# Narrow attention heads on 32-row tiles, their rows gathered through DRAM, and weighted values placed tile by tile

## The chip, the cores and the metric

The kernel runs on one core of a Trainium2 chip. TensorE (PE) multiplies matrices; its weight loads are shown as an engine of their own, PEld. VectorE (DVE), ScalarE (ACT) and GpSimd (POOL) do elementwise work and reductions, SyncE (SP) issues the DMAs. The metric is the device time of one execution in microseconds, lower is better.

## The reference

Four transformer blocks run one after the other on `x` (8 batch elements of 256 tokens of width 128), each with self attention, cross attention to a context of 1601 tokens of width 96, and a feed-forward layer. Blocks 0 and 2 have 16 heads of width 64 ("wide"), blocks 1 and 3 have 16 heads of width 8 ("narrow").

```python
def _attend(q, k, v):                      # block 1; block 3 is alike
    sim = jnp.einsum('bhid,bhjd->bhij', q, k) * HD ** (-0.5)
    attn = jax.nn.softmax(sim, axis=-1)
    out = jnp.einsum('bhij,bhjd->bhid', attn, v)
...
x = x + (_attend(h1 @ Wqkv ...) @ W_proj + b_proj)             # self, 256 keys
x = x + (_attend(h2 @ W_q, ctx @ W_k, ctx @ W_v) @ W_out + b_out)   # cross, 1601 keys
x = x + (gelu(h3 @ W_fc1 + b_fc1) @ W_fc2 + b_fc2)
```

## The kernel before

**Layers and units.** The layers have numbers 0 to 11; attention layers are 0, 1, 6, 7 (wide) and 3, 4, 9, 10 (narrow); 0, 3, 6, 9 are self attention, the others cross attention. Batch elements are taken in pairs (four pairs), and for each layer first the one, then the other. An attention layer of one element is split into units: two wide heads or four narrow heads each, so 8 or 4 units. Keys come in tiles of 128 (2 or 13 of them, the last with 65 rows), and two tiles make a pair. What precedes the units of an element in a layer (projection, norm, feed-forward, keys and queries) is its prelude.

**A unit.** First the jobs "max": the products of queries and keys, in pieces of 400 or 401 keys for cross attention, go to a bank of `ring` (three PSUM banks), and DVE takes each row's maximum into `max_part` (L2042). "shift" turns the maxima into rows that are added inside the score product. Then, chunk by chunk, PE writes `scores` (keys x queries), ScalarE takes the exponential into `probs` (L1719, `exps`), and PE multiplies by the values into `o_acc` (`weigh_values`). ScalarE copies `o_acc` to `attn` at the unit's end ("close"). For wide heads GpSimd adds up the weights (L1271, `add_weights`), for narrow ones a column of ones in the values does.

**Narrow heads.** Queries and keys are held as fp16 high and low halves (`split_of`). A unit's 128 rows in `nk` and `nq` are four blocks of 32 rows: the shift, high x high, low x high, high x low, each with 4 heads x 8 dimensions. SyncE fills blocks 1 to 3 with six DMAs per unit (L1134, L1137, "expand"). GpSimd multiplies the queries by a mask of each head into `qm` (L1290, "mask"), so that a product over all 128 rows gives one head. A score matmul has 128 rows and 512 columns: two heads at once. After "shift" ScalarE copies the shift row into `qm` four times (L1695, `shift_queries`). A chunk is a pair of tiles of two heads.

**Values.** `weigh_values(n, pair)` is one step for a pair of tiles: the heads of a unit go to 32 or 64 columns of the array each, 4 x 2 or 2 x 2 matmuls in fp32, which the trace shows as two instructions each.

**Order of the work.** `make_order` gives each step a due time, and `Plan` replays the steps with assumed durations (`part(engine, stream, due, what, dur, deps, lat)`): each engine takes the due step that is ready. The result is a fixed order for each engine (`ORDER_OF`) and the banks of `ring`. Every engine then runs its list in order.

Of the kernel before, what the change touches and what calls it, by code (L numbers as in the profile page):

```python
# [13 lines left out]
P = 128  # L14
B, N, D = 8, 256, 128
M, DC = 1601, 96
H = 16
# [10 lines left out]
NK_SLOTS, QM_SLOTS, VS_SLOTS = 3, 2, 4  # L28
# [3 lines left out]
class Attention:  # L32
# [170 lines left out]
def make_order():  # L203

    out = []
    begins, ends, expanded, values_at, scores_at, scored, done = {}, {}, {}, {}, {}, {}, {}
# [5 lines left out]
    def place_prelude(s, u, begin):  # L212
# [6 lines left out]
        for m in order:  # L219
# [5 lines left out]
            if kind == "keys" and ATT[s].cross and u % 2:  # L225
                at = max(at, expanded[s, u - 1] + 3.0)
            at += {("ctx", 4): 6.0, ("hn", 1): 5.0, ("ffout", 0): 2.5}.get((kind, j), 0.0)
            put(at, "pre", s, u, m)
            at += AFTER[kind] + (5.0 if kind == "project" and BEFORE[s].wide else 0.0)
# [22 lines left out]
    def place_jobs(un):  # L252
# [6 lines left out]
        if not t.wide:  # L259
# [4 lines left out]
            expanded[t.sub, un.u] = expand  # L264
            put(expand, "expand", n)
            mask = max(expand + 4.5, floor)
            put(mask, "mask", n)
            floor = mask + 0.5
# [45 lines left out]
    for un in UNITS:  # L314
# [48 lines left out]
class Plan:  # L363
# [4 lines left out]
    def __init__(self, static):  # L368
# [3 lines left out]
        for time, i, one in static:  # L372
            place = {"pre": self.pre, "job": self.job, "scores": self.scores, "values": self.values,
                     "close": self.close, "scale": self.scale, "copy": self.copy, "expand": self.expand,
                     "mask": self.mask}[one[0]]
# [6 lines left out]
    def chunk_parts(self, g):  # L382
        un, c = CHUNKS[g]
        out = [("PE", ("values", un.n, c // un.t.halves))]
        if un.t.wide:
            out.append(("POOL", ("values", un.n, c)))
        return out

    def pre(self, due, one):
# [37 lines left out]
        elif kind == "src":  # L427
            old = last_of(s - 3, u - u % 2 + 1)
            on("PE", 0.7, ("PE", ("values", old.n, old.t.pairs - 1)))
            on("ACT", 0.62, pe)  # L430
        elif kind in ("keys", "queries"):
# [3 lines left out]
            spread = [("SP", ("expand", last_of(s, u - 1).n - k)) for k in range(NK_SLOTS)] \  # L435
                if kind == "keys" and t.cross and u % 2 and j == 0 else []
# [68 lines left out]
    def wide_job(self, due, one, un, t, n, j, kind, i, k, pe):  # L505
# [30 lines left out]
        elif kind == "val":  # L536
            back = 2 if t.cross else VS_SLOTS
            deps = self.inputs(un) if i == 0 else []
            if at >= back:
                old = self.wide[at - back]  # L540
                deps.append(("PE", ("values", old.n, old.t.pairs - 1)))
# [7 lines left out]
        else:  # L549
            self.part("PE", "sum", due, one, 0.55, [("POOL", ("values", n, t.pairs - 1))], 0.2)  # L550
# [3 lines left out]
    def narrow_job(self, due, one, un, t, n, j, kind, i, k, pe):  # L554
        if kind == "max":
            self.part("PE", "max", due, one, 0.21 if t.cross else 0.3, [("POOL", ("mask", n)), ("SP", ("expand", n))], 0.2)
# [6 lines left out]
        self.part("PE", "shift", due, one, 0.55, [("DVE", one)], 0.2)  # L563
        self.part("ACT", "shift", due, one, 1.6, [pe])
# [1693 lines left out]
```

## Time and profile before

| | |
|---|---|
| median of 3 runs | 7116.8 us (7109.58 to 7126.71) |
| profiled execution | 7129.41 us, span 7127.6 us |
| PE busy | 6424.0 us, 90% |
| DVE, ACT, POOL busy | 69%, 56%, 38% |
| mean granted TensorE clock | 0.956 |
| moved by DMA | 204.00 MB, 29 GB/s |

A line of the timeline or of a group names the kernel line, the engine, the operation, the tile written and the tiles read, and the shape; for matmuls "128*32" is rows by columns of the array in use. L1309 is the helper `mm` through which nearly all matmuls go, L1593 the copy helper of ScalarE, so such lines are told apart by their tiles: `scores<-qm,nk` are narrow scores, `ring<-nk,qm` the products for narrow maxima, `scores<-qop,...` wide scores, `o_acc<-probs,...` weighted values. Lengths of single matmuls hold the time through the array, and they overlap; the pace is the time from start to start.

### The profile page before, as it was taken

Reading aid. Unit: us, or ns where it says so; the run is one execution under the profiler, and the core shown is the slowest. Engines: PE = TensorE matmul, PEld = TensorE weight load, DVE = VectorE, ACT = ScalarE, POOL = GpSimd, SP = SyncE. Lnnn points to the kernel's source line nnn. Section 1 sums busy time; section 2 is a strip of 40 time slices with the busy share of each in tenths; the row PEclk is TensorE's granted clock in tenths of the full one; section 3 lists DMA queues with packets and bytes.
Section 4 is the critical chain, followed back from the end, with each engine's and each line's share of the span. In section 5 each row is a group of like instructions: output and inputs, shape, how many; then the busy total and the mean of one; then the engine's idle time right before and its main releaser. Section 6 shows DMA issues by size and latency. Waiting matters only on the chain.

```text
span 7127.6 us, 119830 instructions
## 1 busy us (share of the span) xinstructions
PE 6424.0 (90%) x43254; PEld 3725.9 (52%) x43254; DVE 4929.0 (69%) x9886; ACT 3981.7 (56%) x7106; POOL 2707.1 (38%) x2326
## 2 busy tenths in 40 slices
PE   6899889989889998998988999899897999989988
PEld 4555445653455544565455554556444555346644
DVE  6777666657777766665777776666577776766656
ACT  4454565655545557565654555756474445565656
POOL 2446114651144611565014551156401455116630
PEclk9999999999999999999999999999999999999999
DMA  3101011100111001111011100111001010011100
GB/s 81 33 25 26 22 27 32 28 27 18 44 32 27 25 21 31 29 30 29 12 46 31 29 24 20 33 28 30 26 16 46 25 30 24 18 35 28 29 18 11
DMA packets 347633, 204.00 MB, mean 29 GB/s; under 512 B 165006, under 2 KB 319982, under 8 KB 346927
## 3 DMA queue, kind: packets, MB, share of 16 engines
q1 hardware_dynamic: 347054, 196.34, 10.7%
q8 instruction: 357, 5.85, 0.3%
q14 instruction: 222, 1.81, 0.1%
HBM read 105.18 MB, written 1.05 MB: 15 GB/s over the span
## 4 chain that ended last, share of the span: by engine, by line
PE 68%; DVE 12%; ACT 9%; POOL 6%; issue 4%; SPq 1%; DVEq 0%; POOLq 0%; DMA 0%; ACTq 0%
PE ring L1309 34%; PE o_acc L1309 17%; PE scores L1309 16%; DVE max_part L2042 6%; POOL weight_sum L1271 4%; ACT qop L1593 4%; ACT probs L1719 2%; DVE region L2004 1%; DVE o_inv L2073 1%; DVE ring L2021 1%; ACT qm L1593 1%; ACT region L1593 1%; DVE ring L2018 1%; POOL qm L1290 1%; PE ring L1405 1%
## 5 line engine op out<-in xcount | busy, mean ns | idle before, releaser
L2042 DVE TENSOR_REDUCE max_part<-ring 128x1 f32<-128x400 f32 (+2 forms) x4608 | 2454.9, 578 | 829.4 <-PE ring L1309 813.8
L1719 ACT ACTIVATE probs<-scores 128x1024 f32<-128x1024 f32 (+1 forms) x2048 | 1917.6, 969 | 1231.0 <-PE scores L1309 845.3
L1271 POOL TENSOR_TENSOR weight_sum<-weight_sum,probs 128x512 f32<-128x512 f32 (+1 forms) x1408 | 1785.7, 1268 | 143.5 <-ACT probs L1719 2.4
L1309 PE MATMUL o_acc<-probs,region 128*32 128x256 f32 (+2 forms) x13312 | 1360.1, 389 | 0.0
L1271 POOL TENSOR_TENSOR weight_sum<-probs 128x512 f32<-128x512 f32 x256 | 324.8, 1269 | 2125.9 <-PE ring L1309 1794.1
L1593 ACT ACTIVATE region<-ring 64x400 f16<-64x400 f32 (+4 forms) x1744 | 815.0, 477 | 520.5 <-PE ring L1309 416.4
L1309 PEld LDWEIGHTS o_acc<-probs,region 128*32 128x32 f32 (+2 forms) x13312 | 589.0, 123 | 534.0 <-issue 317.9
L1593 ACT ACTIVATE qop<-ring 64x256 f16<-64x256 f32 (+1 forms) x1536 | 563.4, 375 | 446.9 <-DVE ring L2021 278.8
L1309 PE MATMUL scores<-qop,region 128*128 128x256 f16 (+1 forms) x3328 | 781.6, 275 | 12.6 <-ACT probs L1719 8.1
L1309 PE MATMUL ring<-nk,qm 128*128 128x400 f16 (+2 forms) x2560 | 720.6, 343 | 79.2 <-DVE max_part L2042 42.6
L1309 PE MATMUL scores<-qop,x_cop 128*128 128x256 f16 (+1 forms) x3328 | 778.0, 274 | 0.0
L1290 POOL TENSOR_TENSOR qm<-nq,head_mask 128x1024 f16<-128x1024 f16 x128 | 242.1, 1894 | 1129.1 <-PE scores L1309 981.3
L1309 PE MATMUL ring<-region,qop 128*128 128x400 f16 (+1 forms) x2048 | 592.2, 342 | 81.1 <-DVE max_part L2042 46.4
L2004 DVE TENSOR_TENSOR region<-ring,region 64x400 f16<-64x400 f32 (+1 forms) x1024 | 590.5, 577 | 98.8 <-ACT region L1593 74.7
L1309 PE MATMUL scores<-qm,nk 128*128 128x512 f16 (+1 forms) x1920 | 564.9, 385 | 34.7 <-ACT probs L1719 24.5
L2073 DVE RECIPROCAL o_inv<-ring 128x256 f32<-128x256 f32 x256 | 449.8, 1757 | 105.2 <-PE ring L1309 96.3
L1309 PEld LDWEIGHTS ring<-nk,qm 128*128 128x128 f16 x2560 | 222.2, 98 | 571.6 <-DVE max_part L2042 313.3
L1309 PE MATMUL ring<-src_t,stage 96*128 96x400 f32 (+1 forms) x1024 | 439.3, 525 | 33.5 <-ACT qop L1593 32.8
L1309 PEld LDWEIGHTS ring<-region,qop 128*128 128x128 f16 x2048 | 186.7, 98 | 415.7 <-issue 329.7
L1309 PE MATMUL ring<-h_t,stage 128*128 128x256 f32 x1152 | 349.3, 409 | 50.3 <-DVE max_part L2042 10.6
L1309 PEld LDWEIGHTS scores<-qop,region 128*128 128x128 f16 (+1 forms) x3328 | 330.1, 99 | 123.5 <-ACT probs L1719 37.8
L1309 PEld LDWEIGHTS scores<-qop,x_cop 128*128 128x128 f16 (+1 forms) x3328 | 331.3, 100 | 94.1 <-issue 39.8
(159 smaller groups left out, 7449.6 us busy)
## 6 DMA issues: line engine op xcount, KB each, us to landing
x_cop<-region SPq DMA_DIRECT2D x256, 200.1 KB, 3.1
stage<-in_wide SPq DMA_DIRECT2D x512, 64.0 KB, 2.0
nk<-region SPq DMA_DIRECT2D x192, 100.1 KB, 2.2
stage<-in_wide SPq DMA_DIRECT2D x128, 128.0 KB, 2.6
v_stage<-in_wide SPq DMA_DIRECT2D x256, 64.0 KB, 1.8
wo_stage<-in_wide SPq DMA_DIRECT2D x32, 512.0 KB, 4.0
cop_few<-kop_few SPq DMA_DIRECT2D x256, 32.0 KB, 1.9
ff_w<-in_ff_w SPq DMA_DIRECT2D x24, 256.0 KB, 3.1
```

The source lines that it names most:

```text
L1271: pool.tensor_tensor(total, before, probs[0:rows_, g % PROBS, at:at + BANK], ALU.add)\
L1290: pool.tensor_tensor(qm[:, un.narrow_at % QM_SLOTS, :, :], nq[:, z, :].unsqueeze(1).broadcast_to([P, 4, N]), head_mask[:, :].unsqueeze(2). ...
L1309: return pe.matmul(out, lhs, rhs, start=start, stop=stop, skip_group_check=True)
L1405: last = pe.transpose(out[:, p * P:(p + 1) * P], attn[:, p, j * P:(j + 1) * P], ident)
L1593: return act.activation(out, src, ACT.Identity, **kw)
L1719: act.activation(to, src, ACT.Exp, scale=t.scale).then_inc(exp_done.sem, 1)
L2004: last = dve.tensor_tensor(kop[other, h, a0:a0 + w], v[part, 0:w], kop[part, h, a0:a0 + w], ALU.subtract)
L2018: dve.tensor_tensor(v, v, rope_sin[:, a0:a0 + w], ALU.mult).then_inc(rope_step.sem, 1)
L2021: dve.tensor_tensor(v, v, products, ALU.add).then_inc(rope_step.sem, 2)
L2042: dve.tensor_reduce(dst, src, AX.X, ALU.max).then_inc(*release(one))
L2073: dve.reciprocal(o_inv[:, un.wide_at % 2, :], ring[:, bank(one), 0:N]).then_inc(*release(one))
```

## The change

1. A narrow unit's rows are now ordered by head: four heads of 32 rows, each with its four blocks of 8. Each prelude writes its keys and queries to a scratch in DRAM (`key_rows`, `query_rows`; the step "spill", three DMAs each), and "expand" reads a unit's 128 rows from there with two DMAs. The shift blocks of the scratch are written once at the start.
2. A maximum's product and a score product use one head's 32 rows of `nk` and `nq`. Scores of one head fill one bank, so a score step has four matmuls of 256 columns for what were two of 512. The heads of the maxima now change fastest.
3. The mask on GpSimd and `qm` are gone. The shift is added to the queries by three matmuls (a copy of `nq` and the maxima), and ScalarE writes `nq` back in one copy.
4. `weigh_values(n, k)` is a step for one tile of keys, for wide heads too; the adding on GpSimd is a step of its own.
5. Keys of the second element of a pair wait for the spill of the first one's, not for its last "expand". Some assumed durations of `Plan` are new.

```diff
-        out = [("max", (h, q), k) for g in (0, 2) for q in range(QT) for k in range(len(self.kc)) for h in (g, g + 1)]
+        out = [("max", (h, q), k) for q in range(QT) for k in range(len(self.kc)) for h in range(4)]
...
-            put(values_at[n, pair], "values", n, pair)
+            for k in t.tiles(pair):
+                put(values_at[n, pair], "values", n, k)
+            if t.wide:
+                put(values_at[n, pair], "add", n, pair)
...
-            self.part("PE", "max", due, one, 0.21 if t.cross else 0.3, [("POOL", ("mask", n)), ("SP", ("expand", n))], 0.2)
+            self.part("PE", "max", due, one, 0.12 if t.cross else 0.2, [("SP", ("expand", n))], 0.25)
...
-        self.part("PE", "scores", due, one, (0.45 if t.wide else 0.23) * tiles, deps, 0.2)
+        self.part("PE", "scores", due, one, (0.45 if t.wide else 0.13) * tiles, deps, 0.2)
...
-        tiles = len(t.tiles(pair))
-        self.part("PE", "values", due, one, 0.53 * tiles, deps, 0.25)
+        self.part("PE", "values", due, one, 0.53, deps, 0.25)
...
+                    elif one[0] == "spill":
...
+                        rows_ = (query_rows if of_queries else key_rows)[int(t.cross), u % 2, :, :]
+                        rows_ = rows_.rearrange("(h b r) k -> b h r k", b=4, r=8)
+                        for block_, half in zip((1, 2, 3), (0, 0, 1) if of_queries else (0, 1, 0)):
+                            sp.dma_start(rows_[block_, :, :, 0:w], src[:, half, 0:w]).then_inc(done.sem, 16)
...
-                        for block_, of_k, of_q in ((1, 0, 0), (2, 1, 0), (3, 0, 1)):
-                            to = slice(32 * block_, 32 * block_ + 32)
-                            sp.dma_start(nq[to, z, :], q[part, of_q, :]).then_inc(nq_in[z].sem, 16)
-                        for block_, of_k, of_q in ((1, 0, 0), (2, 1, 0), (3, 0, 1)):
-                            to = slice(32 * block_, 32 * block_ + 32)
-                            sp.dma_start(nk[to, z, 0:un.t.keys], k[part, of_k, 0:un.t.keys]).then_inc(nk_in[z].sem, 16)
+                            wait((queries_kept.sem, queries_kept.at((s, u), 48)))
+                            wait((keys_kept.sem, keys_kept.at((s, u), 48)))
+                        part = slice(P * un.p, P * un.p + P)
+                        sp.dma_start(nq[:, z, :], query_rows[int(un.t.cross), u % 2, part, :]).then_inc(nq_in[z].sem, 16)
+                        sp.dma_start(nk[:, z, 0:un.t.keys], key_rows[int(un.t.cross), u % 2, part, 0:un.t.keys])\
+                            .then_inc(nk_in[z].sem, 16)
...
+            wait((init_step, 3))
+            for many in range(2):
+                for z in range(2):
+                    for to, src, w in ((key_rows, nk, MP), (query_rows, nq, N)):
+                        rows_ = to[many, z, :, :].rearrange("(h b r) k -> b h r k", b=4, r=8)
+                        sp.dma_start(rows_[0, :, :, :], src[:, 0, 0:w]).then_inc(blank_in, 16)
...
-                        for q in range(QT):
-                            last = mm(out[0:32, q * P:(q + 1) * P], max_cols[:, q, :], ident, True, True)
+                        mm(out[:, 0:N], ident_half[:, :], nq[:, z, :], True, False)
+                        for q in range(QT):
+                            last = mm(out[:, q * P:(q + 1) * P], max_cols[:, q, :], ident_part[:, :], False, True)
...
-                            last = mm(out[:, m * w:(m + 1) * w], qm[:, un.narrow_at % QM_SLOTS, h, qq * P:(qq + 1) * P],
-                                      nk[:, z, a0:a0 + w], True, True)
+                            last = mm(out[:, m * w:(m + 1) * w], nq[part, z, qq * P:(qq + 1) * P], nk[part, z, a0:a0 + w],
+                                      True, True)
...
-                            last = mm(scores[0:r, first + k % 2, :], nk[:, un.narrow_at % NK_SLOTS, k * P:k * P + r],
-                                      qm[:, un.narrow_at % QM_SLOTS, 2 * half:2 * half + 2, :], True, True)
+                            for h in range(2):
+                                part = slice(64 * half + 32 * h, 64 * half + 32 * h + 32)
+                                at = (k % 2) * N
+                                last = mm(scores[0:r, first + h, at:at + N], nk[part, slot, k * P:k * P + r], nq[part, slot, :],
+                                          True, True)
...
-                    for h in range(4):
-                        last = copy(qm[0:32, un.narrow_at % QM_SLOTS, h, :], ring[0:32, bank(one), 0:N], scale=head_part[0:32, h:h + 1])
-                    last.then_inc(*release(one))
+                    copy(nq[:, un.narrow_at % NK_SLOTS, :], ring[:, bank(one), 0:N]).then_inc(*release(one))
```

The order of PE in a steady narrow cross unit, first before. `ring<-nk,qm` is the product for a maximum, `scores<-qm,nk` half of a score step, `o_acc<-probs,region` weighted values (x8: two tiles of four heads).

```order
L1309 MATMUL o_acc<-probs,region 32x256 x8
L1309 MATMUL ring<-nk,qm 128x400 x3
L1309 MATMUL scores<-qm,nk 128x512 x2
L1309 MATMUL ring<-nk,qm 128x400
L1309 MATMUL scores<-qm,nk 128x512 x2
L1309 MATMUL ring<-nk,qm 128x401
L1309 MATMUL o_acc<-probs,region 32x256 x8
```

And with the change, where `nq` stands for `qm`:

```order
L1318 MATMUL o_acc<-probs,region 32x256 x4
L1318 MATMUL ring<-nk,nq 128x401
L1318 MATMUL o_acc<-probs,region 32x256 x4
L1318 MATMUL ring<-nk,nq 128x401
L1318 MATMUL scores<-nq,nk 128x256 x4
L1318 MATMUL ring<-nk,nq 128x400
L1318 MATMUL scores<-nq,nk 128x256 x4
L1318 MATMUL ring<-nk,nq 128x400
L1318 MATMUL o_acc<-probs,region 32x256 x4
```

The values of a pair now stand as two blocks of one tile, with a maximum's product between them, and a score step is one group of four matmuls.

The order of PE in a unit of the second wide cross layer (7), before and with the change; `ring<-region,qop` are products for wide maxima, the next rows belong to the following units.

```order
L1309 MATMUL o_acc<-probs,region 64x256 x4
L1309 MATMUL ring<-region,qop 128x400
L1309 MATMUL ring<-h_t,stage 128x256
L1309 MATMUL ring<-ctx_t,stage 128x401
L1309 MATMUL ring<-ident,pair_cols 65x128 x2
```

```order
L1318 MATMUL o_acc<-probs,region 64x256 x2
L1318 MATMUL ring<-region,qop 128x400
L1318 MATMUL o_acc<-probs,region 64x256 x2
L1318 MATMUL ring<-h_t,stage 128x256
L1318 MATMUL ring<-ctx_t,stage 128x401
```

Here too a pair's block of four is cut in two by a maximum's product.

The order of SyncE's DMAs where a narrow self layer (3) ends and the cross layer (4) begins, before and with the change.

```order
L1134 DMA nq<-q_split 32x256 x3
L1137 DMA nk<-k_few 32x256 x3
L1134 DMA nq<-q_split 32x256 x3
L1137 DMA nk<-region 32x1601 x3
```

```order
L1137 DMA key_rows<-region 16x8x1601 x3
L1149 DMA nq<-query_rows 128x256
L1150 DMA nk<-key_rows 128x256
L1137 DMA query_rows<-q_split 16x8x256 x3
L1149 DMA nq<-query_rows 128x256
L1150 DMA nk<-key_rows 128x1601
```

The long keys now go out ahead of the last self unit's rows, and the queries go out and come back before the first cross unit's rows are there.

## Rows read from the trace of the kernel before

**Rows 1.** Page, part 1: busy time, share and instructions of each engine.
```profile
PE 6424.0 (90%) x43254; PEld 3725.9 (52%) x43254; DVE 4929.0 (69%) x9886; ACT 3981.7 (56%) x7106; POOL 2707.1 (38%) x2326
```

**Rows 2.** Windows: stretch, its length, then each engine's busy time; granted clock; DMA.
```profile
1993.30:2486.90 493.60, 456.79 (x2924) 279.43 (x2922) 379.38 (x730) 242.99 (x427) 262.76 (x219) 0.99 0.11 28
2486.90:2559.30 72.40, 57.33 (x383) 34.46 (x381) 30.86 (x70) 42.44 (x86) 22.88 (x21) 0.89 0.13 32
2559.30:2772.90 213.60, 201.19 (x1502) 86.17 (x1502) 150.84 (x322) 140.43 (x215) 16.16 (x16) 0.95 0.06 15
2772.90:2888.30 115.40, 98.51 (x616) 63.32 (x616) 82.31 (x154) 71.38 (x163) 28.63 (x32) 0.93 0.17 47
2888.30:3292.40 404.10, 392.24 (x2756) 259.03 (x2755) 263.63 (x474) 239.68 (x419) 266.46 (x220) 0.98 0.11 28
...
2654.50:2674.80 20.30, 19.70 (x168) 7.86 (x168) 16.45 (x34) 14.42 (x20) 1.90 (x1) 1.00 0.09 21
3005.30:3096.40 91.10, 91.10 (x659) 60.02 (x657) 63.45 (x113) 59.22 (x105) 63.47 (x53) 1.00 0.11 28
```

**Rows 3.** Groups by line and shape: busy, mean ns | idle before, releasers.
```profile
L1309 PE MATMUL scores<-qm,nk 128*128 128x512 f16 x1792 | 524.0, 386 | 34.6 <-ACT probs L1719 24.5 <-ACT qm L1593 8.1
L1309 PE MATMUL ring<-nk,qm 128*128 128x400 f16 x1536 | 491.9, 360 | 38.5 <-DVE max_part L2042 19.6 <-DVE ff_h L1918 1.8 <-DVE qop L2001 1.7
L1309 PE MATMUL o_acc<-probs,region 128*32 128x256 f32 x6144 | 411.3, 385 | 0.0
L1309 PEld LDWEIGHTS ring<-nk,qm 128*128 128x128 f16 x2560 | 222.2, 98 | 571.6 <-DVE max_part L2042 313.3 <-issue 127.8 <-POOL qm L1290 27.3
```

**Rows 4.** Timeline of PE in a steady narrow cross unit: start, length, instruction.
```profile
961.03 0.59 PE L1309 MATMUL scores<-qm,nk 128*128 128x512 f16 x2
961.47 0.33 PE L1309 MATMUL ring<-nk,qm 128*128 128x400 f16 x1
961.73 1.07 PE L1309 MATMUL o_acc<-probs,region 128*32 128x256 f32 x16
962.73 0.69 PE L1309 MATMUL ring<-nk,qm 128*128 128x400 f16 x3
963.26 0.59 PE L1309 MATMUL scores<-qm,nk 128*128 128x512 f16 x2
```

**Rows 5.** Timeline of PE, a block of values with one tile.
```profile
2485.84 0.65 PE L1309 MATMUL o_acc<-probs,region 65*64 65x256 f32 x4
2486.42 0.61 PE L1309 MATMUL scores<-qm,nk 128*128 128x512 f16 x2
```

**Rows 6.** Timeline of PE, a matmul of one row behind a maximum.
```profile
2585.95 0.34 PE L1309 MATMUL ring<-nk,qm 128*128 128x400 f16 x1
2586.23 0.71 PE L1309 MATMUL ring<-rows,ones 1*128 1x128 f32 x4
```

**Rows 7.** Timeline of ScalarE and of PE at the end of a narrow unit.
```profile
971.93 1.53 ACT L1593 ACTIVATE qm<-ring,head_part 32x256 f16<-32x256 f32 x4
...
973.52 1.04 PE L1309 MATMUL scores<-qm,nk 128*128 128x512 f16 x4 [0.20 <-ACT qm L1593]
```

**Rows 8.** DMA issues: KB each, median us from issue to landing.
```profile
nk<-region SPq DMA_DIRECT2D x192, 100.1 KB, 2.2
wo_stage<-in_wide SPq DMA_DIRECT2D x32, 512.0 KB, 4.0
```

**Rows 9.** Timeline of SyncE's queue and of PE, first narrow cross unit.
```profile
2550.53 1.98 SPq L1134 DMA_DIRECT2D nq<-q_split  x3
...
2560.30 17.28 PE L1309 MATMUL ring<-nk,qm 128*128 128x401 f16 x36
```

**Rows 10.** Timeline of SyncE's queue after the start.
```profile
43.07 0.90 SPq L1071 DMA_DIRECT2D stage<-in_wide  x2
44.73 1.20 SPq L1119 DMA_DIRECT2D cop_few<-kop_few  x2
```

**Rows 11.** Windows: the stretch with maxima alone.
```profile
2559.30:2580.00 20.70, 19.08 (x47) 5.24 (x47) 18.72 (x41) 1.24 (x5) 0.14 (x1) 0.58 0.08 18
```

More of the change, by code:

```diff
@@ L372, in __init__ @@
         for time, i, one in static:
-            place = {"pre": self.pre, "job": self.job, "scores": self.scores, "values": self.values,
+            place = {"pre": self.pre, "job": self.job, "scores": self.scores, "values": self.values, "add": self.add,
                      "close": self.close, "scale": self.scale, "copy": self.copy, "expand": self.expand,
-                     "mask": self.mask}[one[0]]
+                     "spill": self.spill}[one[0]]
             place((time, i), one)
@@ L383, in chunk_parts @@
         un, c = CHUNKS[g]
-        out = [("PE", ("values", un.n, c // un.t.halves))]
+        out = [("PE", ("values", un.n, un.t.tiles(c // un.t.halves)[-1]))]
         if un.t.wide:
-            out.append(("POOL", ("values", un.n, c)))
+            out.append(("POOL", ("add", un.n, c)))
         return out
@@ L434, in pre @@
             on("PE", 0.7 if kind == "keys" and t.cross else 0.45, *deps)
-            spread = [("SP", ("expand", last_of(s, u - 1).n - k)) for k in range(NK_SLOTS)] \
-                if kind == "keys" and t.cross and u % 2 and j == 0 else []
+            spread = [("SP", ("spill", s, u - 1, 0))] if kind == "keys" and t.cross and u % 2 and j == 0 else []
             on("ACT", 0.62 if kind == "keys" and t.cross else 0.5, pe, *spread)
@@ L549, in wide_job @@
         else:
-            self.part("PE", "sum", due, one, 0.55, [("POOL", ("values", n, t.pairs - 1))], 0.2)
+            self.part("PE", "sum", due, one, 0.55, [("POOL", ("add", n, t.pairs - 1))], 0.2)
             old = [("POOL", ("scale", self.wide[at - 2].n))] if at >= 2 else []
@@ L562, in narrow_job @@
         self.part("DVE", "shift", due, one, 0.2, maxima + ([("PE", ("job", old.n, old.t.shift_job))] if old else []))
-        self.part("PE", "shift", due, one, 0.55, [("DVE", one)], 0.2)
-        self.part("ACT", "shift", due, one, 1.6, [pe])
+        self.part("PE", "shift", due, one, 0.7, [("DVE", one)], 0.2)
+        self.part("ACT", "shift", due, one, 0.4, [pe])
     def scores(self, due, one):
@@ L585, in values @@
     def values(self, due, one):
-        _, n, pair = one
+        _, n, k = one
         un = UNITS[n]
         t = un.t
-        deps = [("ACT", ("scores", un.chunk + pair * t.halves + k)) for k in range(t.halves)]
-        if pair == 0:
+        pair = k // 2
+        deps = [("ACT", ("scores", un.chunk + pair * t.halves + half)) for half in range(t.halves)]
+        if k == 0:
             if t.wide:
@@ L611, in close @@
         un = UNITS[n]
-        deps = [("PE", ("values", n, un.t.pairs - 1))]
+        deps = [("PE", ("values", n, un.t.kt - 1))]
         if un.p == 0 and n:
@@ L625, in copy, with spill @@
         self.part("SP", "copy", due, one, 1.4, [("ACT", ("job", un.n, un.t.last_op))], 2.2)
+    def spill(self, due, one):
+        _, s, u, of_queries = one
+        kind = "queries" if of_queries else "keys"
+        self.part("SP", "spill", due, one, 2.1, [("DVE", ("pre", s, u, of_kind(s, kind)[-1]))], 2.2)
     def expand(self, due, one):
         un = UNITS[one[1]]
-        deps = []
+        s, u = un.t.sub, un.u
+        deps = [("SP", ("spill", s, u, k)) for k in range(2)]
         if un.narrow_at >= NK_SLOTS:
@@ L632, in expand @@
             deps.append(("PE", ("scores", old.chunk + old.t.chunks - 1)))
[L633 to L644 removed]
+        self.part("SP", "expand", due, one, 1.4, deps, 2.2)
     def run(self):
@@ L1716, in exps @@
                         to, src = to[0:r, :, :], src[0:r, :, :]
+                    elif not t.wide:
+                        to, src = to[0:r, :, 0:N], src[0:r, :, 0:N]
                     else:
```

162 lines of the change are left out of this document (74 added, 88 removed).

## The prediction

> **What bounds the kernel now.** I read the page first: TensorE (PE) is busy 90% of 7127.6 us, the next engine, VectorE (DVE), 69% [rows 1]. A share says little about single stages, so next comes the busy time by stage, for the second of four pairs of batch elements [rows 2]. The two cross attentions with wide heads take 493.6 and 404.1 us of it and PE has work for 456.8 and 392.2; in the last row, four units of 22.8 us, PE is busy all the time. A cross attention with narrow heads takes 213.6 us, PE busy 201.2; there are two a pair, so eight in all, with eight units each. In its steady unit of 20.3 us PE is busy 19.7 us and DVE 16.45 us in 34 instructions, 32 of them maxima. That is the floor of such a unit if PE gets cheaper.
>
> Then the parts of a narrow unit on PE. 1792 matmuls of 512 columns (and 128 for the last, short tile) make scores, most of the others feed the maxima with 400 columns [rows 3]. The timeline gives the pace: two score matmuls take 0.44 us to the next start, so 0.215 each, three for maxima 0.53, so 0.17 to 0.18 each, and a block of values of 16 instructions (four heads, two passes of fp32, two tiles of keys) 1.00 us [rows 4]. The four heads overlap: 6144 instructions of mean 385 ns cover 411.3 us [rows 3]. A block costs more than its columns. From the last maximum (0.17) to the block it is 0.26 us: entering the 32-column form costs 0.09 [rows 4]. A block with one tile takes 0.58 us [rows 5], one with two 1.00. So a block cut in two costs 2 x 0.58 - 1.00 + 0.09 = 0.25 us; the one-tile block shown has 64-column tiles, and I use 0.24. Work on 32 rows or fewer has the same entry price: a maximum followed by a matmul of one row is 0.28 us away, not 0.17 [rows 6].
>
> **The change part by part, on PE.**
> (a) Scores of narrow heads. A tile's two heads were one matmul over 128 rows and 512 columns; now they are two matmuls over 32 rows and 256 columns, in different row tiles and PSUM banks. No row of before shows row tiles side by side. Bounds: they overlap as the column tiles do, and a pair costs half, 0.11 for 0.215; or not at all, and it stays 0.22. I take the first, as the nearest row, the four column tiles, does so. 64 units x 26 tile-halves = 1664 matmuls: -1664 x 0.107 = -178 us. The two-tile stages (256 more) are paced by chains, below.
> (b) Values by single tiles. In the order of PE's instructions I count blocks of values: 447 before and 724 after in the narrow cross stages, 816 and 1024 in the wide cross stages, 128 and 228 in the wide self stages, 64 and 76 in the narrow self stages. +277 x 0.24 = +66 us narrow cross; +208 x 0.24 = +50 us wide cross.
> (c) Changes between 32-row work and full-array work (preludes, shifts, the next wide unit's operands): changes of form rise from 3186 to 4920; the blocks of (b) explain 2 x 597 = 1194 of them, of the other 540 some 464 lie in the narrow cross stages: x 0.09 = +42 us.
> (d) Shift of a narrow unit: four instructions of 128 columns become one of 256 more (+0.11 x 64 = +7 us).
> PE in the narrow cross stages: -178 + 66 + 42 + 7 = -63 us.
>
> **What goes beside PE.** ScalarE's four copies after the shift, 1.53 us, become one over 128 rows with as many columns, 0.38 to 0.45. The next scores start right after those copies (0.20 us idle, put down to them) [rows 7], so up to 1.1 us per narrow unit can go, 70 us over 64 units; PE has other work in most of these holes, and I take half, -34. GpSimd's mask goes: the weight loads of maxima waited 27.3 us for it in the whole run [rows 3]; I take -17. Matmuls for maxima next to scores of another row tile can overlap too (up to 0.17 each), but DVE's 16.45 per unit is close below; bounds 0 and, at the floor in all units, -96 more; I take none. Narrow cross: -63 - 34 - 17 = -114 us, or 1.8 per unit: the steady unit goes from 20.3 to 18.5 us, still above 16.45.
> In the wide cross stages nothing pays for (b): the four units at 22.8 us have no hole [rows 2], so the 124 cuts of the second layer count in full (+30), of the first one (84 cuts, PE busy 93%) about half (+10). The wide self stages, PE busy 85% [rows 2]: half of 100 x 0.24, +12.
> Narrow self stages (one takes 72.4 us, PE busy 57.3 [rows 2]): PE waits for chains there. Cheaper: the mask and the copies on ScalarE, and the six issues of SyncE for a unit's rows, 0.6 us each, become two. Dearer: before the first unit the rows go out (three issues, 1.8 us, a landing of 2.2) and in again. Old chain for the first unit: 3.7 of issues + 2.2 of landing, 5.9 us; new one: 1.8 + 2.2 + 1.2 + 2.2 = 7.4, so +1.5 us; with keys of 410 KB the last landing is nearer the 4.0 of a 512 KB one [rows 8], 9.2 in all. In the cross stage that chain starts at 2550.53 and PE's first maximum was at 2560.30, after a turn [rows 9]: 9.8 us hide it. The spill of long keys (3 x 410 KB) also stands in SyncE's order just ahead of the last narrow self unit's rows, which may come 5 us late once per pass and layer (8 x 5 = 40 at worst, 0 at best). I set gains of 3 us per stage against a loss of 3: 0, with -40 and +40 as bounds.
> Start: SyncE reaches its program at 43.07 us and the copy that the first scores need at 44.73 [rows 10]. Eight issues more, at 0.6 to 1.2 each, come ahead of it: +7 us (bounds 5 to 10).
>
> **Sum** against the profiled execution of 7129.4 us: -114 + 40 + 12 + 0 + 7 = -55. That execution is 0.18% above the median of the three runs, 7116.8; 55 less than the median is **7062 us**.
>
> **Two rules of the Trainium skill.** The weight loads of these matmuls took 98 ns, hidden behind matmuls of 170 to 215 ns [rows 3]; now two of them are wanted in 109. The Trainium skill (TensorE: Matmul & The Clock Gate, section "LDWEIGHTS (loading the stationary operand)") says that a load costs by its columns and as much for 32 rows as for 128. By that, were the loads serial, (a) would shrink to nearly nothing; that is rival A. The Trainium skill also says (same page, "Part 3: Packing small matmuls") that loads and matmuls of different row groups overlap, and gives 3.07 times for four row tiles; by that (a) stands. No row of before decides between them.
>
> **Rivals.**
> A, row tiles don't overlap (serial weight loads, or writes to PSUM that exclude each other). For it: nothing in before shows two row tiles at once. Against: 32-column loads and matmuls do overlap. Then (a) is 0 and all switches stay: -55 + 178 = +123, 7240 us, slower. It decides once a pair of 256-column score matmuls takes over 0.14 us: (a) is then 1664 x 0.074 = 123, and the sum 0. Chance 0.15.
> B, the clock falls in the narrow cross stages. In the 20.7 us with only maxima, of 400 columns per 0.485 us, the granted clock was 0.58, between the two levels 1.2 and 2.4 GHz, against 1.00 in the steady unit [rows 2, 11]. Now more of the stage is such thin work on a quarter of the rows. PE's some 17 us of a unit would nearly double at the low level: +16 us; in a third of 56 units +300, 7360 us. Against it: values and scores still stand between, and PE stays busy most of the time. Chance 0.05.
> C, the gain is eaten: DVE is late for each maximum, PE stands in single waits between forms, and the wide cross cuts cost all of their 50. Then narrow cross gives only PE's -63, and the sum is -63 + 50 + 12 + 7 = +6: 7123 us, no change. Chance 0.10.
> D, more than forecast: maxima overlap with scores and the narrow units run at DVE's floor, about 17 us: -96 more, 6966 us. Chance 0.12.
> My forecast, -20 to -100, has 0.58.
>
> **Numbers.** Within 0.2% (14 us), about what a measurement of this kernel can tell from no change: C's 0.10 and little else. Faster: forecast 0.58 + D 0.12 = 0.70, less a bit for the forecast's upper edge: 0.69. Slower: A 0.15 + B 0.05 + 0.01. Together 0.69 / 0.10 / 0.21. The range for 8 in 10 goes down to D with some of what the self stages may add, 6950, and up into the nearer side of A, where tiles overlap in part, to 7200.
>
> **What would show it.** In the profile after: the steady narrow cross unit at 18 to 19 us with DVE over 85% busy; score matmuls of 256 columns in pairs starting some 5 ns apart, a chunk of four in 0.22 us (0.44 by A); two blocks of values per pair of tiles, each 0.55 to 0.6 us; the wide cross stage of 404.1 us longer by some 7 us; granted clock of the steady unit 1.00 (B: under 0.9). The forecast is wrong if the narrow cross stages don't get shorter by 8 us or more each, or if a wide stage grows by more than 15.

## The result

| | median, us | lowest to highest | runs |
|---|---|---|---|
| before | 7121.76 | 7109.58 to 7128.62 | 4 |
| after | 7239.66 | 7229.06 to 7258.08 | 4 |

The ratio is 1.017, 95% interval 1.0144 to 1.0197: the change makes the kernel 118 us slower. The forecast was 7062, its range ended at 7200. The profiled execution of after took 7258.08 us, span 7256.3 us; it is the slowest of its four.

### The profile page after: what moved, and what is told of

Same layout as the page of the kernel before. It is cut to its first block, busy times and chain, and to the rows that moved or that the text cites. A ratio compares the mean times of both kernels' runs of the same rounds, so it can differ in the third digit from the quotient of the medians.

```text
span 7256.3 us, 123089 instructions
## 1 busy us (share of the span) xinstructions
PE 6571.5 (91%) x45302; PEld 3660.9 (50%) x45302; DVE 4929.7 (68%) x9884; ACT 3832.7 (53%) x6722; POOL 2465.1 (34%) x2199
## 4 chain that ended last, share of the span: by engine, by line
PE 69%; DVE 12%; ACT 9%; issue 5%; POOL 4%; SPq 1%; DVEq 0%; POOLq 0%; DMA 0%; ACTq 0%
PE ring L1318 34%; PE o_acc L1318 20%; PE scores L1318 13%; DVE max_part L2056 6%; ACT qop L1614 4%; POOL weight_sum L1294 3%; ACT probs L1736 3%; DVE ring L2035 1%; ACT region L1614 1%; DVE ring L2032 1%; PE ring L1414 1%; DVE o_inv L2087 1%; DVE region L2018 1%; DVE qop L2015 1%; PE ring L1406 0%
## 5 line engine op out<-in xcount | busy, mean ns | idle before, releaser
L1318 PE MATMUL o_acc<-probs,region 128*32 128x256 f32 (+2 forms) x13312 | 1571.4, 432 | 0.0
L1318 PE MATMUL ring<-nk,nq 32*128 32x400 f16 (+2 forms) x2560 | 773.0, 395 | 67.9 <-DVE max_part L2056 42.3
L1318 PEld LDWEIGHTS o_acc<-probs,region 128*32 128x32 f32 (+2 forms) x13312 | 551.1, 129 | 555.0 <-issue 427.6
L1318 PEld LDWEIGHTS ring<-nk,nq 32*128 32x128 f16 x2560 | 199.7, 97 | 717.7 <-issue 333.5
L1257 POOL TENSOR_TENSOR var<-mv,eps 128x2 f32<-128x2 f32 x96 | 18.7, 195 | 1495.5 <-DVE mv L1828 1495.5
L1318 PE MATMUL scores<-nq,nk 32*128 32x256 f16 (+1 forms) x3840 | 383.5, 326 | 33.3 <-ACT probs L1736 20.0
L2015 DVE TENSOR_TENSOR qop<-ring,qop 64x256 f16<-64x256 f32 x512 | 215.5, 421 | 281.7 <-ACT qop L1614 277.6
```

The costliest lines, as they stand in the source:

```text
L1257: pool.tensor_tensor(var[:, :], mv[:, :, 1], eps[:, 0:QT], ALU.add).then_inc(var_ready.sem, 1)
L1318: return pe.matmul(out, lhs, rhs, start=start, stop=stop, skip_group_check=True)
L2015: last = dve.tensor_tensor(qop[part, z, 2 + h, :], v[part, 0:N], qop[part, z, h, :], ALU.subtract)
```

## The profile after

Windows of the kernel after, second pair of batch elements, first the stages of the layers 1, 3, 4, 6 and 7 as in [rows 2], then the eight units of the first of the two narrow cross stages. Columns: stretch, length, busy time of PE, PEld, DVE, ACT, POOL, granted clock, DMA share, GB/s.

```profile
2032.70:2530.40 497.70, 463.92 (x2937) 279.24 (x2934) 379.12 (x731) 244.18 (x426) 260.24 (x218) 0.99 0.11 29
2530.40:2602.70 72.30, 59.47 (x408) 35.75 (x407) 29.53 (x68) 32.19 (x63) 6.71 (x12) 0.76 0.20 58
2602.70:2823.30 220.60, 205.92 (x1680) 77.00 (x1681) 148.33 (x312) 124.31 (x173) 3.31 (x8) 0.76 0.08 24
2823.30:2944.90 121.60, 103.07 (x657) 63.62 (x655) 86.27 (x166) 79.51 (x182) 29.84 (x33) 0.96 0.18 47
2944.90:3347.90 403.00, 394.17 (x2765) 254.17 (x2764) 262.69 (x473) 236.68 (x416) 262.36 (x218) 0.99 0.11 29
...
2602.70:2656.90 54.20, 53.57 (x269) 18.45 (x270) 36.19 (x77) 19.20 (x30) 1.12 (x4) 0.62 0.09 27
2656.90:2682.40 25.50, 24.22 (x215) 8.76 (x213) 17.38 (x37) 15.50 (x26) 0.41 (x1) 0.80 0.21 60
2682.40:2704.80 22.40, 20.94 (x196) 7.28 (x195) 17.61 (x36) 13.35 (x17) 0.00 (x0) 0.77 0.08 24
2704.80:2725.40 20.60, 19.33 (x194) 6.66 (x193) 16.62 (x34) 13.36 (x17) 0.00 (x0) 0.83 0.08 25
2725.40:2753.80 28.40, 26.99 (x219) 11.82 (x218) 18.68 (x44) 16.95 (x23) 0.89 (x2) 0.76 0.07 23
2753.80:2781.20 27.40, 24.16 (x215) 9.13 (x215) 18.35 (x42) 14.73 (x18) 0.89 (x2) 0.75 0.00 1
```

The narrow cross stage, 213.6 us at clock 0.95 in [rows 2], now takes 220.6 at 0.76. The clock has two levels, so a mean of 0.76 is 2 x (1 - 0.76) = 48% of the stretch at 1.2 GHz: 106 us, where it was 22 ("low time" below, taken from the clock's own records and so a little off what the rounded column gives). The steady unit, clock 1.00 before, has 0.77 to 0.83.

Added up over the four pairs, with the stages bounded by the last copy of `o_acc` of each:

| kernel | narrow cross, us (low) | narrow self | wide cross | wide self |
|---|---|---|---|---|
| before | 1692 (155) | 617 (126) | 3593 (111) | 1204 (219) |
| after | 1782 (858) | 615 (254) | 3604 (87) | 1235 (203) |
| difference | +90 | -2 | +11 | +31, of it 7 at the start |

The narrow cross stages carry 90 of 131 us. Stage times are those of one profiled execution of each kernel, and executions of one kernel lie 19 us (before) and 29 us (after) apart, so differences of a few us say little. How one unit looks inside is in the timeline of PE, 12 us of the kernel after; columns: start, length, instruction, and in brackets the idle time before it and what ended it.

```profile
2705.34 0.82 PE L1318 MATMUL ring<-nk,nq 32*128 32x401 f16 x2 [0.50 <-DVE max_part L2056]
...
2707.92 1.70 PE L1318 MATMUL ring<-nk,nq 32*128 32x400 f16 x4
...
2710.64 1.94 PE L1318 MATMUL o_acc<-probs,region 128*32 128x256 f32 x16
2712.51 0.52 PE L1318 MATMUL ring<-nk,nq 32*128 32x400 f16 x2
...
2716.18 0.64 PE L1318 MATMUL o_acc<-probs,region 128*32 128x256 f32 x8
2716.75 0.34 PE L1318 MATMUL ring<-nk,nq 32*128 32x401 f16 x1
2717.02 0.64 PE L1318 MATMUL o_acc<-probs,region 128*32 128x256 f32 x8
2717.59 0.34 PE L1318 MATMUL ring<-nk,nq 32*128 32x401 f16 x1
2717.60 0.39 PE L1318 MATMUL scores<-nq,nk 32*128 32x256 f16 x4
2717.83 0.33 PE L1318 MATMUL ring<-nk,nq 32*128 32x400 f16 x1
```

This is where one unit passes into the next. In the first two rows shown PE gives the next unit's first maxima, on 32 rows, from 2708.14 on one per 0.48 us at the pace of DVE, with scores beside them. At 2708.6 the clock falls and stays low to 2715.4. In between a block of 16 lasts 1.87 us to the next start; it was 1.00 in [rows 4]. From 2716 on, at the upper level, everything has its forecast price: a block of one tile 0.57 us, 0.27 from a maximum to a block, four score matmuls in 0.23. So row tiles do overlap, and a maximum overlaps with scores too (starts at 2717.59 and 2717.60). The Trainium skill (TensorE: Matmul & The Clock Gate, section "Part 3: Packing small matmuls") says that matmuls on different row groups overlap. The trace agrees: four score matmuls on two row tiles take 0.23 us, where the forecast had 0.44 if tiles did not overlap.

That the thin maxima between two units lose the clock is the suspicion with which the experiments begin.

## Experiments

All times are medians, each beside runs of the kernel before on the same chip (7116.5 to 7120.5 us in the three sets). Theory 1: products for maxima on 32 rows lose the clock. Rivals: the cuts of the values and their changes of form (theory 2 below); the plan's new durations; too few columns rather than too few rows.

**e1, values by pairs again.**
```diff
-            for k in t.tiles(pair):
+            for k in t.tiles(pair)[-1:]:
                 put(values_at[n, pair], "values", n, k)
```
(The PE step then places both tiles.)

> The changed kernel with the values placed by pairs of tiles again (one step of TensorE holds both tiles), everything else kept. Theory 1, the clock: the changed kernel is slow because TensorE stands at its lower level for 858 us of the eight narrow cross stages (155 before), and that comes from the products for the maxima, which are not touched here. Then the time at the lower level stays above 1100 us in the whole run (1413 now), the narrow cross stages (1782 us in all) lose at most the 66 us of the cuts, the wide cross stages (3604 us) some 10 to 40 us, and the time is 7150 to 7200. Theory 2, the cuts: 597 blocks of values more and the changes of form around them are what costs. Then the narrow cross stages come back to 1690 or less, and the time to under 7120, whatever the clock does.

Measured 7163.8, ratio to before 1.0059 (1.0044 to 1.0074). The time and the low time of the whole run, 1269 us, are as theory 1 has them; but the narrow cross stages fell by 96 us, to 1686, more than the 66 it allowed, and to just what theory 2 asked for (whose time, under 7120, it missed). Their low time fell by 185 us as well, so this run does not part the two. What it does show is that in the changed kernel the cuts cost 96 us: with pairs, and all maxima still on 32 rows, the narrow cross stages are back where the kernel before has them (1692). The wide cross stages lost 8 us.

**e2, maxima over 128 rows again**, with the mask of queries on GpSimd; scores, single tiles and scratch stay.
```diff
-                            last = mm(out[:, m * w:(m + 1) * w], nq[part, z, qq * P:(qq + 1) * P], nk[part, z, a0:a0 + w],
+                            last = mm(out[:, m * w:(m + 1) * w], qm[:, un.narrow_at % QM_SLOTS, h, qq * P:(qq + 1) * P],
+                                      nk[:, z, a0:a0 + w],
                                       True, True)
...
-            self.part("PE", "max", due, one, 0.12 if t.cross else 0.2, [("SP", ("expand", n))], 0.25)
+            self.part("PE", "max", due, one, 0.21 if t.cross else 0.3, [("POOL", ("mask", n))], 0.2)
```
The second hunk is in the plan: a maximum has its duration of before again and waits for the mask. So PE's order of work is not quite that of the changed kernel (699 blocks of values in the narrow cross stages, not 724).

> The changed kernel with the products for the narrow maxima over all 128 rows of the array again, against queries masked by head on GpSimd; scores on 32 rows, values by single tiles and the scratch are kept. Theory 1, the clock (products over 32 rows, paced by VectorE, do not hold the clock, products over 128 rows do): the time at the lower level in the narrow cross stages falls from 858 us to under 250, and these stages from 1782 us to 1600 to 1680; the time is 7060 to 7150. Theory 2, the cuts: the stages stay at 1780 or grow by the mask and by more changes of form, 7240 to 7300.

Measured 7071.1, ratio 0.9929 (0.9913 to 0.9946): as theory 1 has it, 169 us under the changed kernel, and faster than before, though it adds GpSimd's mask and a change of form at each maximum. Low time in the narrow cross stages 213 us for 858, the stages 1635 us for 1782. Windows of this kernel, the stage and two steady units:

```profile
2550.30:2750.00 199.70, 189.70 (x1692) 71.90 (x1691) 150.13 (x315) 126.81 (x178) 15.95 (x15) 0.95 0.08 23
...
2620.00:2641.30 21.30, 20.20 (x196) 6.55 (x195) 17.97 (x38) 13.39 (x16) 1.89 (x1) 1.00 0.09 27
2641.30:2661.10 19.80, 19.27 (x193) 6.36 (x193) 16.47 (x34) 13.39 (x16) 1.90 (x1) 1.00 0.08 24
```

**e3, each product for a narrow cross maximum twice, on 32 rows.** **e4, one more over 128 rows ahead of each.** In e4 the added line is as below; e3 adds the 32-row product a second time.
```diff
+                            if t.cross:
+                                mm(out[:, m * w:(m + 1) * w], nq[:, z, qq * P:(qq + 1) * P], nk[:, z, a0:a0 + w], True, True)
                             last = mm(out[:, m * w:(m + 1) * w], nq[part, z, qq * P:(qq + 1) * P], nk[part, z, a0:a0 + w],
```

> The changed kernel with each 400-column product for a narrow cross maximum issued twice, both times on 32 rows, into the same bank (the second overwrites the first). If the rows in use decide the clock, the lower level keeps over 700 us of the narrow cross stages, and the time grows by up to 32 x 0.17 us per unit, 7300 to 7600. If it is how many columns pass, or how much of the time TensorE is busy, with 32 rows as good as 128, twice the columns lift the clock: under 300 us at the lower level, and a time of 7150 to 7300, as the second product costs 0.17 us at the upper level and is partly beside VectorE's 0.48.

> The changed kernel with one more 400-column product over all 128 rows ahead of each narrow cross maximum, into the same bank, which the right one on 32 rows overwrites. If the rows in use decide the clock: under 250 us at the lower level in the narrow cross stages (858 now), steady granted clock 0.95 to 1.00 there. The price is TensorE's own: 0.17 us and a change of form of 0.09 to 0.19 us for each of 2048, so 530 to 740 us less what lies in VectorE's shadow: 7300 to 7700. If the rows do not matter, the clock is as in the kernel with the thin product issued twice.

Measured 7466.1 and 7830.7 (one run each). e3 came out as the rows in use would have it: low time 1047 us in the narrow cross stages, so twice the columns on 32 rows don't lift the clock. e4 missed its expectation, with 899 us of low time and a time above the range; its units say more. Windows of e3, units 2 to 4 of the first element, layer 4:

```profile
2714.00:2737.80 23.80, 23.35 (x246) 8.91 (x245) 17.50 (x35) 15.44 (x26) 0.20 (x1) 1.00 0.21 65
2737.80:2764.80 27.00, 26.34 (x230) 9.29 (x229) 17.73 (x35) 13.44 (x16) 0.00 (x0) 0.68 0.07 17
2764.80:2787.00 22.20, 21.54 (x229) 7.95 (x225) 16.76 (x34) 13.50 (x17) 0.00 (x0) 0.85 0.08 24
```
And of e4, the same units and then the units 2 and 3 of the second element, last this unit 3 in the third pair of batch elements:

```profile
2819.90:2849.50 29.60, 29.29 (x242) 11.22 (x241) 18.53 (x35) 15.72 (x26) 0.00 (x0) 1.00 0.15 47
2849.50:2877.40 27.90, 27.90 (x230) 9.72 (x229) 19.16 (x35) 13.58 (x17) 0.00 (x0) 1.00 0.06 19
2877.40:2904.20 26.80, 26.80 (x227) 9.36 (x226) 18.07 (x33) 13.54 (x17) 0.00 (x0) 1.00 0.04 9
...
2934.70:2980.90 46.20, 44.80 (x246) 13.28 (x245) 19.82 (x40) 15.24 (x17) 0.89 (x2) 0.61 0.00 1
2980.90:3028.80 47.90, 47.90 (x232) 11.89 (x232) 20.22 (x36) 13.99 (x16) 0.00 (x0) 0.50 0.00 1
...
4919.80:4948.20 28.40, 28.40 (x233) 9.90 (x232) 19.71 (x36) 13.54 (x16) 0.00 (x0) 1.00 0.01 1
```

In e4 the three units hold 1.00 throughout, here and in all but one of the eight stages. e3 and e4 keep the order of the changed kernel and add the same number of columns, so they compare well. In the units 2 to 4 of the eight stages together the low time is 256 us in the changed kernel, 273 in e3 and 87 in e4. But in e4, once the clock has fallen, it can stay down, for 47.9 us in which PE is busy all the time; the same unit at the upper level took 28.4. So added work over 128 rows kept a clock that was up in these units, and did not bring back one that was down. In e4 PE also has less idle time than in e3, so e4 alone would not show that it is the rows; e2 points the same way with no column added, though in another order of work.

**e5, e2 with pairs.** The edit of e1 on e2.

> The kernel with products for the narrow maxima over 128 rows (7071.1 us), and its values placed by pairs of tiles again. If a block of values cut in two costs TensorE 0.24 us wherever TensorE is the bound, the narrow cross stages (1635 us) lose 20 to 66 us and the wide cross stages (3601 us) 20 to 50: 6960 to 7030. If single tiles cost nothing because they fill waits (the wide cross stages lost only 8 us when the pairs came back to the changed kernel): 7060 to 7085. If pairs are worse, since a longer step of TensorE holds up a product for a maximum: over 7085.

Measured 7072.7, ratio 0.9933 (0.9918 to 0.9948), the middle case in total, but not for its reason: the narrow cross stages became 28 us shorter (1607) and the narrow self stages 2, the wide self stages 27 us longer and the wide cross stages 2. Beside e1 it gives the effect of the maxima's rows a second time, now with pairs: the narrow cross stages go from 1686 us (673 low) to 1607 (252 low).

**e6, e2 with scores over 128 rows as well.**
```diff
-                    copy(nq[:, un.narrow_at % NK_SLOTS, :], ring[:, bank(one), 0:N]).then_inc(*release(one))
+                    for h in range(4):
+                        last = copy(qm[:, un.narrow_at % QM_SLOTS, h, :], ring[:, bank(one), 0:N], scale=head_mask[:, h:h + 1])
+                    last.then_inc(*release(one))
...
+                            last = mm(scores[0:r, first + k % 2, :], nk[:, un.narrow_at % NK_SLOTS, k * P:k * P + r],
+                                      qm[:, un.narrow_at % QM_SLOTS, 2 * half:2 * half + 2, :], True, True)
```

> The kernel with products for the narrow maxima over 128 rows (7071.1 us), and the narrow scores over 128 rows too: two heads in one matmul of 512 columns, the masked queries rewritten by four copies on ScalarE after the shift. Of the change, the scratch, the order of the heads and the single tiles are left. If 32-row score matmuls overlap as forecast (0.11 for two where one of 512 columns took 0.215), the narrow cross stages grow from 1635 us by 100 to 212 us (178 of scores and 34 of copies): 7170 to 7280. If VectorE's pace covers most of it, by 20 to 100: 7090 to 7170. If they bring nothing, under 7085.

Measured 7147.2, ratio 1.0035 (1.0022 to 1.0048): the middle case. 32-row scores and the single copy are worth 35 us in the narrow cross stages (1670 to 1635) beside maxima over 128 rows, and 32 in the narrow self stages (627 to 595). Where the rest of the forecast 212 us stays can be read in the timeline of e2:

```profile
2651.70 0.51 PE L1343 MATMUL ring<-nk,qm 128*128 128x400 f16 x2
2652.15 0.40 PE L1343 MATMUL scores<-nq,nk 32*128 32x256 f16 x8
2652.49 0.34 PE L1343 MATMUL ring<-nk,qm 128*128 128x400 f16 x1
...
2654.18 0.51 PE L1343 MATMUL ring<-nk,qm 128*128 128x400 f16 x2
2654.62 0.39 PE L1343 MATMUL scores<-nq,nk 32*128 32x256 f16 x4
2654.95 0.34 PE L1343 MATMUL ring<-nk,qm 128*128 128x400 f16 x1
```

Eight score matmuls take 0.34 us to the next maximum, four take 0.33. From the second maximum at 2654.36 (start of the group and 0.18) to the one at 2654.95 it is 0.59 us; two of 512 columns and a maximum took 0.44 + 0.17 = 0.61 [rows 4]. A chunk of four alone pays its gain out again in two changes of form; only two chunks in a row gain.

**e7, the kernel before with values by single tiles**, nothing else (the hunks on `weigh_values` and `add` of the diff above).

> The kernel before with the values placed by single tiles, nothing else. By the forecast's price of 0.24 us a cut the wide cross stages (3593 us) grow by 40, the wide self stages (1143 us) by 12 and the narrow cross stages (1692 us) by up to 66 us: 7170 to 7240. If single tiles fill waits and cost nothing, as the wide stages of the changed kernel have it: 7105 to 7140.

Measured 7150.2, ratio 1.0040 (1.0025 to 1.0055), between the two cases. By stage: narrow cross +1, wide cross -1, narrow self -4, wide self +27 (the medians +30). The steady wide cross unit grew as forecast, but in layer 7 the second unit of the stage shrank. Windows of before, layer 7, second and third unit of the stage:

```profile
2925.60:2959.70 34.10, 30.86 (x179) 19.40 (x180) 21.37 (x38) 18.21 (x35) 17.67 (x15) 0.85 0.07 19
2959.70:2982.50 22.80, 22.80 (x167) 15.04 (x166) 15.89 (x29) 14.83 (x28) 15.87 (x14) 1.00 0.11 28
```

The same two units of e7:

```profile
2934.50:2960.40 25.90, 25.19 (x174) 16.02 (x174) 17.32 (x32) 15.53 (x29) 15.03 (x14) 1.00 0.09 25
2960.40:2983.70 23.30, 23.30 (x166) 14.86 (x165) 15.83 (x29) 14.65 (x27) 15.85 (x14) 1.00 0.11 27
```

+0.5 us in each steady unit, -8.2 in that one, with its clock from 0.85 to 1.00. The clock is not all of that: 0.85 over 34.1 us is 10 us of low time, worth 5 us at most by the ratio of the two levels. And it is no rule. In layer 1 the second unit of the stage grew by 4 us with the same edit, and its clock fell. Windows of before and of e7:

```profile
2035.20:2072.10 36.90, 31.15 (x191) 19.13 (x189) 28.74 (x66) 17.25 (x30) 12.99 (x13) 0.95 0.18 45
...
2040.50:2081.40 40.90, 34.57 (x193) 20.66 (x193) 29.10 (x66) 17.29 (x30) 15.02 (x14) 0.87 0.16 40
```

**e8, e2 with pairs for narrow heads only** (the best of the stages so far, put together).

> The kernel with products for the narrow maxima over 128 rows (7071.1 us), with values by pairs of tiles for narrow heads and by single tiles for wide ones. In the kernel with pairs everywhere the narrow cross stages were 28.6 us shorter (1606.7 against 1635.3), the wide self stages 27 us longer (1246 against 1219). If each of the two belongs to its own stage: 7035 to 7055. If the wide self stages move with any change in the order of the work (they lie between 1203 and 1250 us in the kernels run so far, with pairs and with single tiles), it comes out anywhere between 7040 and 7080.

Measured 7054.9, ratio 0.9907 (0.9891 to 0.9924), within both cases. Narrow cross 1597 us, narrow self 588; wide self 1242, though its values are single tiles as in e2 (1219). It is the fastest kernel of this study, 62 us under before.

**e9, maxima on 32 rows with scores over 128** (e6 without the mask, the products for the maxima as in the change).

> The fourth of a square: products for the maxima on 32 rows as in the changed kernel, scores over 128 rows, two heads in one matmul, as before; the queries of each head are written by four scaled copies on ScalarE, without the mask; scratch and single tiles as in the changed kernel. If the maxima on 32 rows lower the clock by themselves: 500 to 900 us at the lower level in the narrow cross stages (137 with both over 128 rows, 213 with thin scores alone, 858 with both thin), and a time of 7200 to 7290, 50 to 140 above the kernel with both over 128 rows (7147.2). If it takes both to be thin, since scores over 128 rows hold the clock: under 300 us at the lower level, and 7120 to 7170.

Measured 7418.6, ratio 1.0419 (1.0403 to 1.0434). The square of low times in the narrow cross stages is complete:

| narrow cross, us (low) | scores on 32 rows | scores over 128 |
|---|---|---|
| maxima on 32 rows | 1782 (858) | 1964 (519) |
| maxima over 128 | 1635 (213) | 1670 (137) |

Maxima on 32 rows cost the clock with either form of the scores; thin scores add to it. Between the two rows of the table the plan's duration of a maximum changes too (0.12 and 0.21 us), and with it PE's order; e10 looks at that. The upper row also shows what thin scores and the single copy are worth beside thin maxima: 182 us, though the low time rises by 339. The clock came out as expected, the time 130 us above its range. The clock is not all of it: the second unit, at 1.00 in both, takes 22.6 us here and 21.7 in e6. More changes of form between maxima and scores could do that; it was not measured apart.

**e10, the change with the plan's durations of before.**
```diff
-            self.part("PE", "max", due, one, 0.12 if t.cross else 0.2, [("SP", ("expand", n))], 0.25)
+            self.part("PE", "max", due, one, 0.21 if t.cross else 0.3, [("SP", ("expand", n))], 0.25)
...
-        self.part("PE", "scores", due, one, (0.45 if t.wide else 0.13) * tiles, deps, 0.2)
+        self.part("PE", "scores", due, one, (0.45 if t.wide else 0.23) * tiles, deps, 0.2)
```

> The changed kernel with the durations before the change in the plan that sets the order: 0.21 us for a product for a narrow cross maximum instead of 0.12, 0.23 instead of 0.13 a tile for narrow scores. If the new, shorter durations spread the work badly and that is what lowers the clock: under 500 us at the lower level in the narrow cross stages (858 now), and 7080 to 7160. If the rows in use do it, whatever the order: 700 to 950 us at the lower level, and 7210 to 7270.

Measured 7339.8, ratio 1.0306 (1.0289 to 1.0322), low time 1099 us: outside both cases. With the durations of before it got worse, so the new durations are not the cause; but the order alone moves the low time of the narrow cross stages by 241 us and the stages from 1782 to 1866, more than was expected. Its units show what the clock costs. Windows of e10, units 2 to 4, first pair, and then unit 4 of the second pair:

```profile
852.70:869.70 17.00, 16.40 (x189) 6.12 (x187) 15.47 (x33) 11.87 (x16) 0.00 (x0) 1.00 0.15 37
869.70:895.20 25.50, 23.71 (x191) 7.08 (x188) 16.30 (x33) 13.28 (x18) 0.00 (x0) 0.60 0.08 22
895.20:921.90 26.70, 25.32 (x194) 7.63 (x193) 16.43 (x34) 13.28 (x18) 0.00 (x0) 0.55 0.07 19
...
2722.00:2740.60 18.60, 16.45 (x194) 6.16 (x193) 16.19 (x35) 13.34 (x18) 0.00 (x0) 1.00 0.08 25
```

The last two rows are the same unit, with the same matmuls: 26.7 us at clock 0.55 and 18.6 at 1.00, so 8.1 us for 24 us of low time, 0.34 for each. 18.6 us is what the forecast gave a steady unit (18.5); unit 2, at 17.0 in two of the eight stages, comes to what rival D had. What the change offers is there, and the clock takes it.

## Why the prediction was wrong

The step that failed is the one on rival B: "values and scores still stand between, and PE stays busy most of the time", chance 0.05. PE does stay busy (205.9 of 220.6 us), and the clock fell all the same. [rows 11] had shown half of it: maxima alone, over 128 rows at the same pace of 0.485 us, already ran at a mean of 0.58. With maxima on 32 rows the clock also falls inside the stage, between two units, with scores standing between (0.83 in the steady unit). That maxima on 32 rows do this is shown by three pairs of kernels: low times of 858 and 213 us (after, e2), 519 and 137 (e9, e6), 673 and 252 (e1, e5). In all three the order of work changes a little too, and only e3 and e4 hold it fixed. e3 rules out the number of columns. Whether the rows in use are all that counts is not shown beyond these runs. B was also priced wrongly: I gave 16 us to a third of the units. Measured, most units have 7 to 17 us of low time (the first of a stage 28 to 47, the last often none), and what e2 takes off (645 us of low time) went with 147 us of time, 0.23 us for each, and the unit of e10 has 0.34. Between levels of 1.2 and 2.4 GHz it can be up to half. That DVE's pace covers part of PE's slowness would explain the rest; it was not tried. At 0.23 to 0.34 the 703 us of low time more in the narrow cross stages are, as an estimate, 160 to 240 us, and forecast and measurement of these stages (-114 and +90) lie 204 apart.

The measured time is that of rival A, 7240, but its mechanism did not happen: four thin scores take 0.23 us. A number that fits is no evidence for the mechanism behind it.

By term, in the narrow cross stages:
- (a) scores -178 and the copies -34: about as large in the change as it was made, with maxima on 32 rows too: -182 (e9 to after), in spite of the low time; part of it may be changes of form that e9 has between its maxima and scores. With maxima over 128 rows only -35 is left (e6 to e2); there a lone chunk between two maxima gives its gain back at two changes of form.
- (b) cuts +66: the price at the upper level is right (0.57 and 0.27 us), but the sum depends on what stands around. Measured -96 when they go from the changed kernel (after to e1), with 185 us of low time that I had not counted; +28 with maxima over 128 rows (e5 to e2); +1 in the kernel before (e7), which has 181 cuts for the 277 forecast.
- (c) changes of form +42: no run has it apart.
- Where e2 stands, 1635 us, is 57 below before for the forecast 114.

Elsewhere: wide cross +40, measured +11 (after) and -1 (e7). In layer 7 the steady unit grew by 0.5 us, as 124 cuts in 64 units make it, but the second unit of a stage lost 7 to 9 us, a term I did not have; in layer 1 the steady unit grew by 0.2 and the second by 4. Wide self +12, measured 24 besides the start. It grew by 15 to 46 us in nine of the ten kernels of the experiments, the start included, with pairs or without; only e9 was 3 under before. I know of no single cause, and it was not tried apart: any new order of the work seems to lose what the order before had there. Narrow self 0, measured -2: there the low time doubled (126 to 254) and hid a gain, since e2 has -22. Start +7: SyncE's first issue of its program was at 43.07 us [rows 10], and is here in after:

```profile
49.91 0.90 SPq L1076 DMA_DIRECT2D stage<-in_wide  x2
```

6.8 us later, as forecast. The chain through the scratch stayed hidden: PE's first narrow cross maximum starts 2.0 us after the stage's bound (1.0 before).

## What to carry to other kernels

When a matmul is made to use fewer rows, price the clock as well as the pace: look at the granted clock in the stretches where it waits for another engine, not at its mean busy share, and ask what is left there. Price a cut or a new order in the kernel that will have it: much the same cuts cost 96 us beside maxima on 32 rows and 28 beside maxima over 128. Small matmuls side by side only pay in runs of the same form; one alone between others gives the gain back at both ends. And a mixed design was better than either pure one: thin scores, products for the maxima over all rows, pairs for the narrow values, 0.9% under the kernel before.

## What the runs showed of the hardware

- Products of the same columns hold the clock less well on 32 rows than over 128: 858 against 213 us at the lower level in the eight narrow cross stages (after, e2). Twice as many of them on 32 rows did not help (1047 us, e3).
- A clock once low can stay low while TensorE is busy without a gap: 47.9 us at 0.50 in e4, with products over 32 and over 128 rows taking turns; the same unit at the upper level took 28.4 us.
- Matmuls on four different 32-row tiles overlap: eight of 256 columns take 0.34 us from their first start to the next product over 128 rows (e2), four on two tiles 0.33. A product on 32 rows and the scores behind it start within 10 ns (after). Between a product over 128 rows and one on 32, either way, there are 0.09 to 0.1 us that do not overlap (e2).
- The order of work alone moves the time at the lower level: 858 to 1099 us in the narrow cross stages from after to e10, and with blocks of values cut in two the second wide cross unit went from 0.85 to 1.00 in layer 7 and from 0.95 to 0.87 in layer 1 (e7).
